# The ternary weights in thirteen pieces beside the second half of the first pair, in place of two blocks beside its first half

## The reference, cut to what matters

```python
def cross_attention_0(x, context):          # 8 heads of 64, 1024 queries, 6404 keys
    q, k, v = x @ Wq, context @ Wk, context @ Wv
    return softmax(q @ k.T / 8) @ v @ Wo + bo

def bitnet_linear(x, W, b):                 # W_d2v, W_img, W_txt, W_att0, W_att1, W_f1, W_f2
    w_scale = maximum(mean(abs(W)), 1e-5)
    qW = sign(W) * (abs(W) > 0.5 * w_scale)         # -1, 0 or 1
    i_scale = maximum(max(abs(x)), 1e-8) / 127
    qx = clip(round(x / i_scale), -128, 127)
    return qx @ qW.T * (w_scale * i_scale) + b
```

## Time and profile before

| | us |
|---|---|
| three timed runs, median | 1729.21 (1724.82 to 1729.83) |
| the profiled execution | 1728.0 |
| its span, first to last instruction | 1726.3 |
| PE busy | 1516.9 (88% of the span) |
| DVE busy | 1291.2 (75%) |
| ACT busy | 1118.8 (65%) |
| POOL busy | 433.0 (25%) |
| half 0 of the attention loop | 127.20 |
| half 1 | 123.51 |
| half 2 | 111.44 |

### The profile page before, as it was taken

One profiled execution on the slowest core, in us unless ns is written; L12 is line 12 of the kernel. 1 busy time (PEld: TensorE's weight loads), 2 busy tenths in 40 slices (PEclk: granted clock), 3 DMA queues, 4 the chain that ended last, 5 costly groups with the idle time before them and its releaser, 6 DMA issues.

```text
span 1726.3 us, 26028 instructions
## 1 busy us (share of the span) xinstructions
PE 1516.9 (88%) x8864; PEld 542.1 (31%) x8864; DVE 1291.2 (75%) x2214; ACT 1118.8 (65%) x1496; POOL 433.0 (25%) x413
## 2 busy tenths in 40 slices
PE   3878889999999999999999997899996869978963
PEld 2412223333333333333332333343333612311312
DVE  4798688777888778887789898766665676778775
ACT  3687667776777767867767686655553466746633
POOL 5401333343443434433400010344441000000000
PEclk7966889999999999999999998999998958986986
DMA  4000000000000000000010000111100000000000
GB/s 127 7 0 6 1 1 2 1 1 1 8 1 1 1 1 3 1 1 10 20 32 1 1 1 22 32 41 46 41 27 0 1 0 1 1 1 1 1 13 12
DMA packets 12556, 20.26 MB, mean 12 GB/s; under 512 B 1670, under 2 KB 11254, under 8 KB 12342
## 3 DMA queue, kind: packets, MB, share of 16 engines
q1 hardware_dynamic: 12438, 18.76, 3.9%
HBM read 18.23 MB, written 0.52 MB: 11 GB/s over the span
## 4 chain that ended last, share of the span: by engine, by line
PE 64%; DVE 14%; issue 13%; POOL 5%; ACT 3%; DMA 1%; POOLq 0%; SPq 0%; ACTq 0%; DVEq 0%
PE PS L1744 26%; PE PS L1729 18%; PE PS L1776 4%; POOL WRK L599 4%; DVE KNB L1078 4%; PE PS L1692 3%; PE PS L1619 2%; PE PS L1611 2%; DVE WRK L1128 1%; DMA KNB<-in_ctx_fm_dram 1%; DVE QS L1134 1%; PE PS L2020 1%; PE PS L2005 1%; ACT KNB L758 1%; ACT WRK L738 1%
## 5 line engine op out<-in xcount | busy, mean ns | idle before, releaser
L1128 DVE TENSOR_TENSOR WRK<-WRK 128x768 f32<-128x768 f32 (+1 forms) x500 | 550.4, 1101 | 57.2 <-ACT WRK L738 45.1
L738 ACT ACTIVATE WRK<-PS 128x1024 f32<-128x1024 f32 (+1 forms) x510 | 500.0, 1022 | 104.9 <-PE PS L1729 90.7
L1744 PE MATMUL PS<-WRK,V 128*64 128x512 f32 (+1 forms) x2040 | 498.0, 608 | 0.0
L1078 DVE CUSTOM_DVE_ANT_0 KNB<-PS,KNB 128x512 f16<-128x512 f32 (+2 forms) x464 | 331.4, 731 | 150.9 <-PE PS L1776 139.0
L572 POOL TENSOR_TENSOR WRK<-WRK 128x256 f32<-128x256 f32 x300 | 277.8, 926 | 411.7 <-ACT WRK L738 394.5
L758 ACT ACTIVATE KNB<-PS 128x512 f16<-128x512 f32 (+2 forms) x306 | 181.1, 592 | 108.3 <-PE PS L1776 108.2
L1916 PE MATMUL PS<-WRK,KNB 128*128 128x512 f16 x828 | 198.1, 384 | 11.0 <-POOL WRK L599 4.3
L1744 PEld LDWEIGHTS PS<-WRK,V 128*64 128x64 f32 (+1 forms) x2040 | 124.3, 136 | 247.8 <-issue 199.1
L1729 PE MATMUL PS<-Q,KB 64*128 64x512 f16 (+1 forms) x1428 | 192.7, 379 | 0.5 <-ACT WRK L738 0.4
L1729 PE MATMUL PS<-KNB,KB 64*128 64x512 f16 (+1 forms) x1224 | 156.3, 377 | 0.0
L599 POOL TENSOR_TENSOR WRK<-KB,WRK 128x1024 f16<-128x1024 f32 x46 | 98.6, 2143 | 133.9 <-ACT WRK L884 133.9
(11 more groups left out here) (333 smaller groups left out, 1501.0 us busy)
## 6 DMA issues: line engine op xcount, KB each, us to landing
V<-in_moe_w_dram SPq DMA_DIRECT2D x44, 192.0 KB, 2.4
KNB<-in_ctx_fm_dram SPq DMA_DIRECT2D x1, 2401.5 KB, 18.5
CTX<-in_ctx_fm_dram SPq DMA_DIRECT2D x6, 384.0 KB, 4.4
BW<-in_bit_w_dram SPq DMA_DIRECT2D x1, 960.0 KB, 6.2
PWK<-in_pair_w_dram SPq DMA_DIRECT2D x4, 192.0 KB, 2.6
SM<-in_small_dram SPq DMA_DIRECT2D x1, 716.5 KB, 4.6
XT<-in_x_fm_dram SPq DMA_DIRECT2D x1, 512.0 KB, 5.5
X<-in_x_tm_dram SPq DMA_DIRECT2D x1, 512.0 KB, 7.4
```

Source lines behind the costliest of these rows:

```text
L738: e.activation(PR[0:r, u % 2, b, :], bank(2 * b, 2 * b + 2, slice(0, r)), ACT.Exp).then_inc(S("exp"), 1)
L1078: return e.tensor_tensor_reduce(diffs, sums, diffs, 0.5, NEG, ALU.add, ALU.max, accum_out=out)
L1128: e.tensor_tensor(total, total, part, ALU.add).then_inc(S("acc"), 1)
L1744: ins = e.matmul(PS[h * HD:(h + 1) * HD, 4, :], v(r, j, h), PR[0:r, unit_no(hf, i) % 2, b, h * HALF:(h + 1) * HALF], start=(j == 0), stop= ...
```

## The change

Two things change. POOL's all-reduce is issued after the adds of unit 12 of half 1 (slot 38 of pair 0) in place of unit 8 of half 0 (slot 8). And the two DVE blocks become thirteen pieces, one in a slot, at the same place in the slot: the sums in slots 34 to 37, the scales in slot 40, the first comparison in 41 to 43, the second in 44 to 46, the copies for att0 and att1 in 47 and 48. The instructions are the same; one wait, between those that make `BH` and `BN`, is gone. No DMA moves.

```diff
-BIT_AT = {6: "bit_sums", 12: "bit_weights"}
+
+BIT_AT = {34: ("sum", 0, 3), 35: ("sum", 3, 5), 36: ("sum", 5, 6), 37: ("sum", 6, 7), 40: ("scale",), 41: ("low", 0, 5),
+          42: ("low", 5, 6), 43: ("low", 6, 7), 44: ("high", 0, 5), 45: ("high", 5, 6), 46: ("high", 6, 7),
+          47: ("pairs", 0), 48: ("pairs", 1)}
...
-                    if hf == 0 and i == 8:
+                    if hf == 1 and i == 12:
                         e.wait_ge(S("bit_rows"), 1)
                         e.partition_all_reduce(BT[:, 0:7], BR[:, 0:7], P, RED.add).then_inc(S("bit_sum"), 1)
...
+            def weights(a, b):
+                return [(i, slice(BIT[n_][0], BIT[n_][0] + BIT[n_][1])) for i, n_ in enumerate(BIT_N) if a <= i < b]
+
+            def bit_step(kind, a=None, b=None):
+                if kind == "sum":
+                    if a == 0:
+                        e.wait_ge(S("ld_bit"), 32)
+                    for i, cols in weights(a, b):
+                        ins = e.tensor_reduce(BR[:, i:i + 1], BW[:, cols], X, ALU.add, apply_absolute_value=True)
+                    if b == len(BIT_N):
+                        ins.then_inc(S("bit_rows"), 1)
+                elif kind == "scale":
+                    e.wait_ge(S("bit_sum"), 1)
+                    for i, nme in enumerate(BIT_N):
+                        ins = e.tensor_scalar(BS[:, i:i + 1], BT[:, i:i + 1], 1.0 / BIT[nme][3], 1e-5, ALU.mult, ALU.max)
+                    link(ins)
+                    e.tensor_scalar(BH[:, 0:7], BS[:, 0:7], 0.5, None, ALU.mult)
+                    link(e.tensor_scalar(BN[:, 0:7], BS[:, 0:7], -0.5, None, ALU.mult))
+                elif kind == "low":
+                    for i, cols in weights(a, b):
+                        ins = e.tensor_scalar(BQ[:, cols], BW[:, cols], BN[:, i:i + 1], None, ALU.is_lt)
+                    link(ins)
+                elif kind == "high":
+                    for i, cols in weights(a, b):
+                        ins = e.scalar_tensor_tensor(BQ[:, cols], BW[:, cols], BH[:, i:i + 1], BQ[:, cols], ALU.is_gt,
+                                                     ALU.subtract)
+                    link(ins)
+                else:
+                    e.tensor_scalar(B2[:, a:a + 1], sm(f"b_att{a}"), 2.0, None, ALU.mult)
+                    w = BQ[:, 384 + 64 * a:448 + 64 * a]
+                    for k in range(2):
+                        e.tensor_scalar(BQN[:, a, k * HD:(k + 1) * HD], w, -1.0, None, ALU.mult)
+                        ins = e.tensor_copy(BQD[:, a, k * HD:(k + 1) * HD], w)
+                    if a:
+                        ins.then_inc(S("bit_q"), 1)
...
                     if p == 0 and s in BIT_AT:
-                        (bit_sums if BIT_AT[s] == "bit_sums" else bit_weights)()
+                        bit_step(*BIT_AT[s])
```

More of the change, by code:

```diff
@@ L1184, in bank5 @@
                     add_out(a)
[L1186 to L1215, removed]
```

## The result

The changed kernel takes 1716.6 us (median of 7 runs, 1714.54 to 1720.62), the one before, timed beside it, 1727.26 (7 runs, 1724.82 to 1729.83). The ratio is 0.9941, with a 95% interval of 0.9930 to 0.9953: 10.2 us less, between 8.1 and 12.1. The profiled execution has a span of 1718.1 us, against 1726.3.

What follows compares the result with a forecast made beforehand. It took half 0 to have holes and half 1 to be bounded by PE's work, with 27 us of DVE free. The terms -20.7 + 7.6 + 1.3 = -11.8 us gave 1717.4 us, range 1711.5 to 1722.5.

Steps and rivals of the forecast that it cites:

- The removed terms: Half 0: taking out the sums, the all-reduce and the ternary block saves 1.66 + 9.2 + 9.85 = 20.7 us.
- the sums: Half 0: seven reductions on DVE, 2.64 us long, had lengthened two slots by 1.66 us.
- the all-reduce: Half 0: POOL's 13.5 us pause had cost 9.2 us, 5.5 from ACT's delay and 3.7 from the low clock.
- the ternary block: Half 0: 8.4 us on DVE that no slot can hide, with a second clock fall, had cost 9.85 us.
- The all-reduce in half 1: Half 1: the same 13.5 us pause makes ACT 3.9 us late and the low clock adds 3.7, sum 7.6 us.
- The rival without a fall: Half 1: the clock stays up behind the shorter PE gap, saving 3.7 us, 1713.7 us; chance 0.20.
- DVE waiting for the all-reduce: Half 1, scale in slot 40: all-reduce ends before DVE gets there, 1.0 us to spare, cost 0.
- The pieces: Half 1, slots 34 to 48: the thirteen DVE pieces cost 1.3 us, bounds 0 and 5.
- The tolerances: Half 1: lateness DVE may have before PE waits for its maximum, 0.57 us for odd-slot pieces, 2.43 for even-slot ones.
- The price of being held by POOL: Half 1: DVE pieces held by a POOL add cost up to 0.55 us each, about 0.8 in all.
- The low clock stayed: Rival: behind the pause PE runs at 0.50 through the rest of half 1, about 1750 us; chance 0.04.
- the rival of exposed pieces: Half 1: DVE becomes the bound; pieces exposed by half (1722 us, chance 0.11) or nearly in full (1727.1, chance 0.08).

Runs made afterwards that it cites:

- the repeated profiles: The unaltered changed kernel and the kernel before, each profiled once more: half 1 of the changed one 131.35 us against 132.38, half 0 of the one before 125.66 against 127.16.
- early_all_reduce: Changed kernel with the sums ahead of the loop and the all-reduce right behind the kernel's first one: half 1 125.87 us, ratio to the kernel before 0.9903.
- no_all_reduce: Changed kernel without the all-reduce, scales made from each partition's own sums: half 1 126.43 us, ratio to the kernel before 0.9903.
- small_even: Sums and all-reduce ahead of the loop, remaining ternary work in smaller blocks in even slots 34 to 48: half 1 123.44 us, ratio to the kernel before 0.9888.

## Why the prediction was right, point by point

The forecast was 1717.4 us and the measured median 1716.6, a change of -11.8 against one of -10.2 (8.1 to 12.1). That the two times agree to 0.8 us is partly luck: the forecast started from a median of 1729.21 for the kernel before, and seven runs gave 1727.26. From there it would have been 1715.5. The steps held unequally.

- **The removed terms.** I had 20.7 us, and half 0 got 19.57 shorter (17.6 between the repeated profiles). By the lateness of the exps, the sums had cost 1.64 us (forecast 1.66), the all-reduce 8.26 (9.2) and the ternary block 9.82 (9.85). The mis-sized term is in the all-reduce: a slot's natural length. I had taken slot 11 at 4.56 us (4.23 and a third maximum step at 0.33). The kernel after shows it undisturbed, from the value matmuls at 199.89 to those at 205.41, 5.52 us: the third step brings not only two matmuls, but also waits of PE for DVE's maxima (0.27 and 0.44 us in the rows). For the same reason the 3.7 us that I had charged to the low clock was too high; in half 0 of before it added 2.9.

```profile
199.89 1.94 PE L1752 MATMUL PS<-WRK,V 128*64 128x512 f32 x8
...
203.07 0.39 PE L1784 MATMUL PS<-KNB,Q 64*128 64x512 f16 x2 [0.27 <-DVE MXP L1081]
...
204.55 0.39 PE L1784 MATMUL PS<-KNB,Q 64*128 64x512 f16 x2 [0.44 <-DVE MXP L1081]
...
205.41 1.94 PE L1752 MATMUL PS<-WRK,V 128*64 128x512 f32 x8
...
209.11 1.94 PE L1752 MATMUL PS<-WRK,V 128*64 128x512 f32 x8
```

- **The all-reduce in half 1.** 7.6 us forecast, 7.59 measured over slots 40 to 43, but of other parts than I said. The pause was 14.5 us and not 13.5 (the instruction took 1.24 us, not 0.49, and the idle parts 0.2 more), and the last add ahead of it ended 0.3 us later after the exp of unit 38. So ACT was late by 4.8 us and not 3.9. The low clock lasted 6.8 us and not 10, and added 2.3 and not 3.7. The other 0.5 is the lateness behind the piece of slot 43, which `early_all_reduce` shows without a pause too. So 0.9 and 0.5 us too little and 1.4 too much cancel here, and the repeated profile, where these slots cost 6.6 us, shows the agreement to be luck. That the clock falls behind a gap of about 4 us was right in every profile that had one (3.83, 4.17, 4.22, 4.30 and 4.39 us). The rival without a fall never occurred. The prediction has PE at work for about 10 us of both low stretches of half 0; the second (222.2 to 232.4) lies half inside PE's gap (220.2 to 227.5).
- **DVE waiting for the all-reduce.** Expected with 1.0 us to spare; there were 0.2, since the all-reduce ended 10.8 us after the exp of unit 38 and not 9.7. Right, but nearly wrong.
- **The pieces.** 1.3 us forecast, 1.40 measured outside slots 40 to 43. By place the two agree less: the sums cost 0.55 us, where 0.1 was reckoned, and the slots from 44 on 0.85. That those of slots 40 to 42 were free behind the pause was right, to 0.2 us: without the pause they cost 1.1. As a price of thirteen pieces 1.3 would have been wrong by more than half, as `no_all_reduce` with its 3.03 shows. The tolerances, 0.57 us ahead of an even slot and 2.43 ahead of an odd one, were the right idea: 1.40 against 6.22 us for the same blocks. As numbers they were rough. Some blocks came out longer than I had split them, even slots don't all tolerate the same (slot 40 against slot 36), and a block of 5.1 us brought in the clock.
- **The price of being held by POOL.** L1198 took 0.72 us before; its successor took 0.17 in the kernel after, where POOL was in its pause, and 0.72 in `small_even`, beside a POOL add:

```profile
308.09 0.73 POOL L576 TENSOR_TENSOR WRK<-WRK 128x256 f32<-128x256 f32 x1 [0.18 <-ACT WRK L739]
...
308.12 0.72 DVE L1208 TENSOR_SCALAR BH<-BS 128x7 f32<-128x7 f32 x1
```

  Both times that it took 0.72 us it ended within 0.03 us of a POOL add. The five small comparisons of slot 41 took 1.75 us while POOL caught up, where 0.9 was expected. The Trainium skill ("SBUF — State Buffer", section "SBUF: two separate sides") has the port pair of the two engines locked for a whole instruction, against a VectorE operation in a two-port mode or with two SBUF inputs; the rows agree, but don't show the mode. What it cost the changed kernel, no run here separates from the rest.
- **The argument itself.** The prediction began from half 0 having holes and DVE having 27 us free in half 1. The runs show another reading: pieces in half 0 gain nearly as much (-10.3 against -10.6). The sum came out since it was made item by item. DVE's free 27 us carried no number of it; they stood against the rival of exposed pieces, and were no argument there: the same six blocks cost 6.2 us in odd slots and 1.4 in even ones.
- **The rivals.** None came true as a whole, though pieces were held as L1198 was. The low clock stayed for 6.8 us, far from the 34 from which it would have decided.

## What to carry to other kernels

Ask of a side job on a fast engine how long one uninterrupted item of it is and which wait stands behind it, not how much idle time the engine has: the same scales, comparisons and copies, some 8.4 us of DVE or a little more beside POOL's adds, cost 7.6 us as one item and 7.1 as two (both with a fall of the clock), 6.2 as six in odd slots, 1.4 as six in even ones and 0.0 as eight smaller ones. Read the tolerance from the distance between the end of the result and the start of the instruction that needs it, and keep each item well inside it. And look for a place where an operation that makes an engine change its kind of work, like the all-reduce among adds, disturbs nobody: moving it to where POOL was idle anyway was worth another 6 us.

## What the runs showed of the hardware

- POOL's change from adds to a partition all-reduce cost 5.7 to 6.1 us of idle time and the change back 6.7 to 7.3 us, in every profile here, and the same whether one or two all-reduces stand between.
- PE gaps of 1.5, 1.8 and 1.9 us in the loop left the granted clock at 1.00; gaps of 3.83 us and more brought it to 0.50 every time, for 3.4 to 10.2 us, and for different times in two profiles of the same kernel.
- An operation on seven elements took 0.17 us on DVE alone and 0.72 beside a POOL add of 0.73 us, and the same seven comparisons took 2.06 us in two kernels and 2.71 in a third. That POOL's adds made the difference there too is likely and not shown.
- Halves 2 to 6 of the loop repeat to 0.02 us from kernel to kernel, and so does half 1 up to its first ternary piece, so that one profile prices an item to 0.1 us where the clock stays up. It doesn't where the clock falls (1 to 1.5 us), in the first units of half 0 (0.7 us), or ahead of and behind the loop (6.4 and 3.9 us).
